# Five of the eight mask additions of batches 2 and 3 move from VectorE to GpSimd in an mLSTM stage

## The reference, cut to what matters

```python
logfg = jax.nn.log_sigmoid(f_pre)
Fcum = jnp.cumsum(logfg, axis=-1)
Dmat = Fcum[..., :, None] - Fcum[..., None, :] + i_pre[..., None, :]
Dmat = jnp.where(causal, Dmat, -jnp.inf)
m = jnp.max(Dmat, axis=-1, keepdims=True)
Smat = jnp.exp(Dmat - m)
C = qk * Smat
n = jnp.maximum(jnp.abs(jnp.sum(C, axis=-1, keepdims=True)), jnp.exp(-m))
h = einsum(C / n, v)
h_norm = h * rsqrt(mean(h * h) + EPS) * mh_w      # per head of 32 features
x1 = x + (sigmoid(o_pre) * h_norm) @ w_out
```

## Time and profile before

| | |
|---|---|
| median of 3 runs | 669.71 us (668.55 to 671.12) |
| profiled execution | 667.9 us, of which the span is 666.1 us |
| TensorE busy | 652.1 us (98% of the span) |
| VectorE busy | 438.7 us (66%) |
| ScalarE busy | 411.3 us (62%) |
| GpSimd busy | 245.9 us (37%) |
| TensorE's granted clock, mean | 0.996 |

### The profile page before, as it was taken

The page is one execution under the profiler, slowest core; times in us unless marked ns, Lnnn a source line. Parts: engine busy times, 40 slices in busy tenths (PEclk is TensorE's granted clock), DMA queues, the critical chain, the costliest instruction groups (busy, mean ns, idle before and its releaser), DMA issues. The chain is left out here.

```text
span 666.1 us, 14564 instructions
## 1 busy us (share of the span) xinstructions
PE 652.1 (98%) x4961; PEld 611.0 (92%) x4961; DVE 438.7 (66%) x952; ACT 411.3 (62%) x1085; POOL 245.9 (37%) x279
## 2 busy tenths in 40 slices
PE   8999999999999999999999999999999999999995
PEld 8998998999998999989988999999986799999995
DVE  6566666666765665775675676556569986556877
ACT  5566676666866666866676864333689964333553
POOL 3735482033370250650374545112452462122101
PEclk9999999999999999999999999999999999999998
DMA  8265555426635345545165104000157100000000
GB/s 286 72 200 161 170 162 154 135 85 189 185 100 154 78 143 185 148 135 153 53 209 159 45 2 167 17 0 9 44 192 267 56 1 1 1 1 0 1 33 31
DMA packets 38171, 69.72 MB, mean 105 GB/s; under 512 B 3440, under 2 KB 22640, under 8 KB 37872
## 3 DMA queue, kind: packets, MB, share of 16 engines
q1 hardware_dynamic: 37696, 68.38, 33.5%
q10 hardware_dynamic: 432, 0.79, 0.4%
HBM read 52.18 MB, written 16.97 MB: 104 GB/s over the span
## 5 line engine op out<-in xcount | busy, mean ns | idle before, releaser
L332 PE MATMUL PJ<-xTh,WBh 128*128 128x256 f32 (+1 forms) x252 | 87.7, 348 | 0.0
L333 PE MATMUL PJ<-xTl,WBh 128*128 128x256 f32 (+1 forms) x252 | 83.6, 332 | 0.0
L334 PE MATMUL PJ<-xTh,WBl 128*128 128x256 f32 (+1 forms) x252 | 83.5, 331 | 0.0
L933 POOL TENSOR_TENSOR stage<-stage 128x256 f32<-128x256 f32 x32 | 24.6, 768 | 140.8 <-DVE stage L794 140.5
L688 ACT ACTIVATE probs<-probs,rinv 128x256 f32<-128x256 f32 x128 | 58.3, 506 | 22.1 <-DVE rinv L816 21.9
L948 POOL TENSOR_TENSOR WBl<-raw,WBh 128x512 fp32r<-128x512 f32 x32 | 40.7, 1296 | 61.8 <-ACT WBh L705 61.8
L805 DVE TENSOR_TENSOR QKl<-PJ,QKh 128x512 fp32r<-128x512 f32 x60 | 41.4, 690 | 25.8 <-ACT QKh L676 25.5
L334 PEld LDWEIGHTS PJ<-xTh,WBl 128*128 128x128 f32 x252 | 47.7, 189 | 5.0
L1174 POOL TENSOR_SCALAR vare<-mv 128x2 f32<-128x2 f32 x13 | 2.9, 224 | 132.5 <-DVE mv L1167 132.5
L332 PEld LDWEIGHTS PJ<-xTh,WBh 128*128 128x128 f32 x252 | 48.0, 190 | 2.9
L333 PEld LDWEIGHTS PJ<-xTl,WBh 128*128 128x128 f32 x252 | 48.0, 191 | 2.3
(11 more groups left out here) (348 smaller groups left out, 2515.8 us busy)
## 6 DMA issues: line engine op xcount, KB each, us to landing
K<-scr_k SPq DMA_DIRECT2D x60, 256.0 KB, 4.4
raw<-in_w_att SPq DMA_DIRECT2D x37, 256.0 KB, 4.8
Q<-scr_q SPq DMA_DIRECT2D x15, 512.0 KB, 6.7
stage<-scr_m SPq DMA_DIRECT2D x6, 768.0 KB, 4.3
scr_q<-rot_h SPq DMA_DIRECT2D x30, 128.0 KB
scr_q<-rot_l SPq DMA_DIRECT2D x30, 128.0 KB
scr_k<-rot_h SPq DMA_DIRECT2D x30, 128.0 KB
scr_k<-rot_l SPq DMA_DIRECT2D x30, 128.0 KB
```

The costliest lines, as they stand in the source:

```text
L332: pe.matmul(out, ah, bh, start=(i == 0), stop=False)
L333: pe.matmul(out, ah, bl, start=False, stop=False)
L334: last = pe.matmul(out, al, bh, start=False, stop=(i == n - 1))
```

## The change

GpSimd makes the mask additions of batch 2's quarters 0, 1 and 2 ahead of `head_scales(0)`, and those of batch 3's quarters 0 and 1 behind it. VectorE keeps quarter 3 of batch 2 (after pair (1, 3)) and quarters 2 and 3 of batch 3 (after pairs (2, 2) and (2, 3)). Both sides add to the one counter `masked_rows`, so each waits at a handover until the other has reached its number: GpSimd for 8 ahead of batch 2 and 12 ahead of batch 3, VectorE for 11 ahead of (2, quarter 3) and 14 ahead of (3, quarter 2). `quarter_blocks` and `mask_blocks` are the operands as before, given names.

```diff
+        mask_blocks = mask[:, :].rearrange("p (a b n) -> p a b n", a=1, b=1).broadcast_to([P, 2, 2, P])
+        def quarter_blocks(c, quarter):
+            return A[c % 2][:, 2 * quarter:2 * quarter + 2, :].rearrange("p h (b n) -> p h b n", n=P)[:, :, 0:3:2, :]
...
# VectorE, mask_rows
                     dve.wait_ge(a_half[c % 2][quarter // 2], 16 if c == 1 else 32)
-                a = A[c % 2][:, 2 * quarter:2 * quarter + 2, :].rearrange("p h (b n) -> p h b n", n=P)[:, :, 0:3:2, :]
-                m = mask[:, :].rearrange("p (a b n) -> p a b n", a=1, b=1).broadcast_to([P, 2, 2, P])
-                dve.tensor_tensor(a, a, m, ALU.add).then_inc(s_["masked_rows"], 1)
+                if (c, quarter) in ((2, 3), (3, 2)):
+                    dve.wait_ge(s_["masked_rows"], HM // 2 * c + quarter)
+                a = quarter_blocks(c, quarter)
+                dve.tensor_tensor(a, a, mask_blocks, ALU.add).then_inc(s_["masked_rows"], 1)
...
# VectorE, the loop over pairs
-                    if c in (1, 2):
+                    if (c, pair) in ((1, 3), (2, 2), (2, 3)):
                         mask_rows(c + 1, pair)
...
# GpSimd
             pool.wait_ge(s_["xs_ready"], N_RMS[1] + 4)
+            def mask_rows(c, quarters):
+                pool.wait_ge(s_["masked_rows"], HM // 2 * c)
+                for quarter in quarters:
+                    pool.wait_ge(a_half[c % 2][quarter // 2], 32)
+                    a = quarter_blocks(c, quarter)
+                    pool.tensor_tensor(a, a, mask_blocks, ALU.add).then_inc(s_["masked_rows"], 1)
             split_mlp(0, 12)
+            pool.wait_ge(s_["small_in"], 64)
+            mask_rows(2, (0, 1, 2))
             head_scales(0)
+            mask_rows(3, (0, 1))
```

## The result

The changed kernel takes 673.48 us (median of 9 runs, 671.16 to 680.23), the kernel before 669.02 us in the same comparison (9 runs, 667.89 to 671.12): ratio 1.0071, 95% interval 1.0048 to 1.0094. It is slower by 0.7%: 4.5 us between the medians, 4.7 by the ratio. The profiled execution took 672.31 us with a span of 670.3, against 667.9 and 666.1 before: +4.2 us in the span. The forecast was +1.3.

A forecast was written before the change was run, and what follows sets the result against it. No engine bounds the heads' stage by itself; the order of hand-overs does. -0.3 - 0.6 + 1.1 + 1.1 = +1.3 us on 669.7 gives 671.0, no measurable difference (within 0.5%, chance 0.84), range 668.5 to 673.0.

The forecast's parts named there:

- Where the masks are free: Masks at pairs (1, 0), (1, 1), (2, 1), each alone behind its `weigh`: worth 0, VectorE's idle 0.20 us becoming 0.8.
- The earlier power: Without VectorE's mask at 512.96 beside GpSimd's L2166, the power ends 0.32 us earlier, on the path: -0.3 us.
- the mask behind `norm_b(0)`: Quarter 0 of batch 3, between `norm_b(0)` and `weigh` (2, 1), leaves the chain that ended last: -0.6 us.
- the -0.9 of the working: The gain of the masks leaving VectorE, taken alone: -0.3 for the power and -0.6 for the mask behind `norm_b(0)`.
- GpSimd's time: Five additions on GpSimd at 1.30 us each; batch 2's three end by about 511.7, 0.8 us before `head_scales(0)`: worth 0.
- rival 4: GpSimd's additions longer than 1.30 us from strided blocks and repeated mask, holding up `head_scales(0)`: +3.0, 672.7 us; chance 0.08.
- The collision: In `norm_b(0)`, GpSimd's two batch 3 additions block VectorE's operations with two SBUF inputs: +1.1 us twice.
- the engines take turns in order of arrival: GpSimd's second addition, queued before VectorE's second multiplication in `norm_b(0)`, goes first: a second +1.1 us.
- rival 1: VectorE keeps its turn through `norm_b`, blocked only by the first addition: +0.2, 669.9 us; chance 0.20.
- rival 2: No contention at all, or GpSimd's additions come behind `norm_b`: the 0.9 gain stands, 668.8 us; chance 0.13.
- rival 3: TensorE's clock halves in the gap ahead of `heads_T(0)`, scores +0.7 us a pair: +3.4 to +5.5, 674.2 us; chance 0.15.
- The gap that I had worked out: TensorE standing still ahead of `heads_T(0)`, from about 518.25 to 520.1: some 1.8 us, against a longest wait of 0.74.

The follow-up runs named there:

- experiment 3: The changed kernel with only batch 2's three additions on GpSimd, all four of batch 3 on VectorE: 668.02 us against 668.1 for the kernel before, ratio 0.9994.
- experiment 1: The changed kernel with GpSimd's two additions of batch 3 waiting until `norm_b(0)` is done: 666.7 us against 668.1 for the kernel before, ratio 0.9982.
- experiment 6: As experiment 3, plus GpSimd zeroing two unused 128x512 blocks by memset behind the power: 668.61 us in a single run.
- experiment 4: The changed kernel with only batch 3's two additions on GpSimd, batch 2's on VectorE: 673.06 us against 668.1 for the kernel before, ratio 1.0067.
- experiments 7 and 8: The kernel before with two or three scans of unread data on VectorE in `norm_b(0)`: 670.45 us, ratio 1.0034, and 674.4 us, ratio 1.0075.
- experiment 2: The changed kernel with seven more unread matmuls on TensorE ahead of `heads_T(0)`: 669.54 us against 668.1 for the kernel before, ratio 1.0017.
- experiment 7: The kernel before with two scans of unread data on VectorE in `norm_b(0)`: 670.45 us against 668.43, ratio 1.0034.

## Why the prediction was wrong

**Where the masks are free: right.** Three of the five masks were priced at nothing and VectorE's idle time behind them grew from 0.20 to 0.80 us, as forecast. The earlier power (-0.32 in experiment 3) and the mask behind `norm_b(0)` (-0.6 more in experiment 1) gave the -0.9 of the working.

**GpSimd's time: right.** 3.74 us for three, 1.29 for one without a block, so rival 4 has no ground: the strided blocks and the repeated mask cost nothing, and `head_scales(0)` wasn't late.

**The collision: right, in mechanism and size.** Two blocks of about 1.07 us instead of 1.1. The step that I had only read out of one cast at 409.80, that the engines take turns in order of arrival, held: rival 1 (VectorE keeps its turn) and rival 2 (no contention) fall by the rows of L2028. The rule as the prediction tells it, that whoever is first keeps the shared pair for the whole instruction, fits the additions; the power and the mask beside it (experiment 6) show that it doesn't fit every instruction that reads SBUF. `weigh` (2, 1) was forecast at 520.05 and came at 520.04; net +1.23 against the +1.3 of the sum.

**The clock: the step that failed.** The sum ended with the blocking and put the clock at nothing; it stood outside as rival 3 with a chance of 0.15. It measured 2.9 us in the profiled execution, more than the whole +1.2 of the rest. The gap that I had worked out (1.8 us) was right (1.76), and the text had already set it beside the 1.8 us after which the clock fell at the kernel's end. What I held against it, that the stage kept 1.00 through its many short waits and that TensorE works right ahead of the gap and behind it, says nothing about a longer gap: no wait over 0.74 us was in the trace of the stage. In this stage the clock fell at 1.76 and 2.13 us of standing still (the latter in experiment 4) and behind the pairs of waits of experiments 7 and 8 (0.75 and 0.81, 1.32 and 0.81); it held with waits of up to 0.74 and, in experiment 2, with the 1.76 filled. The mean granted clock of the changed kernel's nine runs is 0.974 to 0.991, in all of them below the lowest of the kernel before in the experiments' comparisons (0.993), so it seems to have fallen every time.

**Rival 3's own price** was 4.5 us (674.2 on 669.7) and the loss is 4.5 in the medians, 4.1 in the stage. That it fits is partly luck. I had priced the scores alone, 0.7 us a pair, and let the low clock last three to six pairs. It lasted two, but all of TensorE's work takes 1.6 to 2 times as long in them, and with `project_out` TensorE is itself the bound: +0.4 for the first pair and +2.6 for the second.

## What to carry to other kernels

Before moving work to GpSimd, look at what VectorE does in the instant in which GpSimd gets to it. If both were released by the same operation they start together, and an operation of VectorE with two SBUF inputs then waits for GpSimd's turn, once for each addition that is queued; a wait that puts the work behind VectorE's critical operations costs nothing if there is slack (experiment 1). And a microsecond that a change adds to TensorE's longest wait is not a microsecond: work out the new gap, compare it, together with any wait that follows close behind, with the longest over which the clock has held in the trace, and beyond it price the following stretch at half the clock, everything that TensorE does there. Here 0.75 us was enough once a second wait of 0.81 came right behind. An unread matmul or a few in the gap bound that risk.

## What the runs showed of the hardware

- GpSimd and VectorE alternate instruction by instruction when both queue for SBUF reads: additions of 1.29 and 1.46 us interleaved with multiplications of 1.50 and 1.48 us that take 0.42 alone. GpSimd's memset didn't take part, and its power of 128x16, 2.92 us long, didn't block a mask of two SBUF inputs (0.68 us).
- The low clock, once there, doesn't end with the gap: it lasted 6.8 us in the changed kernel and behind two scans, 10.2 us in experiment 4 and 17.1 us behind three scans, with TensorE shown as busy nearly all of that time. In the last case the stage came out 8.6 us longer, of which only 1.8 lay ahead of the fall.
- Two waits of 0.75 and 0.81 us with 0.66 us of transposes between them came ahead of the fall in the profiled execution of experiment 7; in four of its ten runs the mean clock shows no fall in the stage.
